# Expert stage of a fused attention, FFN and mixture-of-experts kernel: gated units split before their transpose, down product one tile later

## What is computed

```python
logits = x2d @ gate_kernel                     # 2048 rows, 32 experts
weights, chosen = top_k(softmax(logits), 8)    # weights normed to sum 1
# rows sorted by expert; for the rows of expert e:
inter = silu(rows @ gate_proj[e]) * (rows @ up_proj[e])     # 512 -> 192
out_rows = inter @ down_proj[e]                             # 192 -> 512
x = x + sum over the 8 chosen experts of weight * out_rows
```

## Time and profile before

| what | before |
|---|---|
| runs | 1450.37, 1451.21, 1453.27 us (median 1451.21) |
| span of the profiled execution | 1474.3 us |
| PE busy, share of the span | 1382.7 us, 94% |
| DVE, ACT, POOL busy | 69%, 34%, 26% |
| mean granted TensorE clock | 0.977 |
| DMA | 345.04 MB, 234 GB/s mean |

### The profile page before, as it was taken

How to read it: one execution, slowest core, us unless ns; L and a number is a source line. 1 busy time by engine, 2 the same in 40 slices (tenths; PEclk the granted TensorE clock), 3 DMA queues, 4 the chain that set the end, 5 groups by cost and what they waited for, 6 DMA issues and landing times.

```text
span 1474.3 us, 26984 instructions
## 1 busy us (share of the span) xinstructions
PE 1382.7 (94%) x7525; PEld 753.2 (51%) x7526; DVE 1022.1 (69%) x2467; ACT 505.4 (34%) x916; POOL 383.7 (26%) x313
## 2 busy tenths in 40 slices
PE   4799999999999999999999559999999999999997
PEld 3344444444444444455444236666666666666664
DVE  7879857976895656688776536666666666666664
ACT  1454543444435343422222113333333333333332
POOL 1000000000000000025556543444344344344443
PEclk9899999999999999999999769999999999999999
DMA  9975776766767778836748668889999888989785
GB/s 370 396 262 193 263 256 213 247 197 205 241 209 237 235 254 286 280 119 251 284 195 294 242 227 216 223 218 260 246 246 234 221 229 228 247 223 222 148 162 84
DMA packets 132696, 345.04 MB, mean 234 GB/s; under 512 B 15008, under 2 KB 19616, under 8 KB 125728
## 3 DMA queue, kind: packets, MB, share of 16 engines
q1 hardware_dynamic: 73488, 206.72, 41.6%
q0 software_dynamic: 34640, 85.74, 25.2%
q10 hardware_dynamic: 24512, 51.89, 10.8%
HBM read 192.68 MB, written 151.62 MB: 234 GB/s over the span
## 4 chain that ended last, share of the span: by engine, by line
PE 68%; DVE 16%; DMA 4%; issue 4%; ACT 3%; another core or an unknown queue 2%; ACTq 1%; SPq 1%; DVEq 0%; POOLq 0%
PE PS L1671 17%; PE PS L1673 17%; PE PS L1672 17%; PE PS L1933 5%; PE PS L1961 2%; PE PS L1962 2%; DMA split_experts<-HT 2%; DMA CST<-in_kv 1%; PE PS L1950 1%; DVE EX L1300 1%; PE PS L1951 1%; DVE EX L1306 1%; DVE nw L1027 1%; DMA X<-in_x 1%
## 5 line engine op out<-in xcount | busy, mean ns | idle before, releaser
L587 POOL DMA_INDIRECT out<-BIG,EX x159 | 247.2, 1555 | 354.9 <-issue 153.4
L1671 PE MATMUL PS<-BIG 128*128 (+1 forms) x795 | 269.5, 339 | 5.0 <-DVE BIG L1572 3.3
L1672 PE MATMUL PS<-BIG 128*128 (+1 forms) x795 | 269.5, 339 | 0.0
L1673 PE MATMUL PS<-BIG 128*128 (+1 forms) x795 | 269.5, 339 | 0.0
L1671 PE MATMUL PS<-HT,BIG 128*128 128x512 f16 (+1 forms) x512 | 194.1, 379 | 3.0 <-DVE HT L1101 1.4
L1672 PE MATMUL PS<-HT,BIG 128*128 128x512 f16 (+1 forms) x512 | 194.0, 379 | 0.0
L1673 PE MATMUL PS<-HT,BIG 128*128 128x512 f16 (+1 forms) x512 | 194.0, 379 | 0.0
L560 POOL DMA_INDIRECT rows_by_expert<-HT,POS x128 | 124.9, 976 | 122.6 <-DVE POS L1391 88.1
L1672 PE MATMUL PS<-BIG,EX 128*128 128x512 f16 (+1 forms) x376 | 143.8, 382 | 1.1 <-issue 1.1
L824 ACT ACTIVATE BIG<-PS 128x256 f16<-128x256 f32 x159 | 61.1, 384 | 243.3 <-PE PS L1951 229.0
L1673 PE MATMUL PS<-BIG,EX 128*128 128x512 f16 (+1 forms) x376 | 143.6, 382 | 0.4 <-issue 0.4
(11 more groups left out here) (264 smaller groups left out, 2218.0 us busy)
## 6 DMA issues: line engine op xcount, KB each, us to landing
BIG<-rows_by_expert ACTq DMA_DIRECT2D x159, 280.0 KB
HT<-in_experts SPq DMA_DIRECT2D x64, 640.0 KB, 4.6
BIG<-split_experts SPq DMA_DIRECT2D x32, 1152.0 KB
split_experts<-HT SPq DMA_DIRECT2D x96, 320.0 KB, 2.2
CST<-in_kv SPq DMA_DIRECT2D x64, 256.0 KB, 4.7
split_context<-RT SPq DMA_DIRECT2D x64, 256.0 KB, 4.5
BIG<-split_context SPq DMA_DIRECT2D x7, 2048.0 KB
rows_by_expert<-X SPq DMA_DIRECT2D x32, 280.0 KB
```

Source lines behind the costliest of these rows:

```text
L587: pool.indirect_dma_start(a_out, bass.IndirectOffsetOnAxis(ap=IDY[:, u % V:u % V + 1], axis=0), yt[u % V], None, compute_op=ALU.add).then_ ...
L1671: mm(out, lh, rh, start=first, stop=False)
L1672: mm(out, lh, rl, start=False, stop=False)
L1673: return mm(out, ll, rh, start=False, stop=last_group)
```

## The change

The units are split before they are transposed. `hidden` writes 192 columns once; ACT writes their hi part and DVE their lo part in SBUF (`hidden_hi`, `hidden_lo`), arranged in three blocks of 128 fp16 columns: hi of units 0 to 127; hi of 128 to 191 beside lo of 128 to 191; lo of 0 to 127. PE transposes these three blocks in fp16, and ACT copies them from PSUM to SBUF in one instruction (`hidden_copy`). In `tile_down` the fourth matmul multiplies the stacked middle block with hi weights in both partition halves, and the fifth has 64 rows only. So the last 512 weight columns are kept as hi and as lo (E16 is 5120 columns, 1280 KB per expert), and `split_half` is the same for both halves.

PE's step becomes rows of t + 3, gate and up of t + 2, units of t + 1, down of t. LEAD is 7. ACT's start mixes silu, hi parts and early loads. SP writes eight pads before its loop. `load_counts` reads a table like `load_ints` and takes the maximum with the least value on each register.

```diff
-EL = KC * GU + D
-E16 = EW + EL
+E16 = 2 * EW
-LEAD = 6
+LEAD = 7
+def load_counts(eng, name, table, least, most):
+    loaded = [eng.alloc_register(f"{name}{i}") for i in range(table.shape[-1])]
+    held = [eng.alloc_register(f"{name}_held{i}") for i in range(table.shape[-1])]
+    eng.reg_load(loaded, table)
+    for to, of in zip(held, loaded):
+        eng.reg_alu(to, of, least, ALU.max)
+        eng.free_register(of)
+    return [eng.snap(x, donate=True, min_val=least, max_val=most) for x in held]
...
             def store_half(e, h):
-                nl = (EH, EL - EH)[h]
-                sp.dma_start(dst[:, EW + h * EH:EW + h * EH + nl], eol[:, 0:nl]).then_inc(s_eo, 16)
+                sp.dma_start(dst[:, EW + h * EH:EW + (h + 1) * EH], eol).then_inc(s_eo, 16)
...
-            for e in range(WP):
+            for e in range(2 * WP):
                 pad_expert(e, 16 * e)
             sp.wait_ge(s_tab, 1)
-            with sp.Fori(1, NE // WP) as i:
+            with sp.Fori(1, NE // WP - 1) as i:
                 for h in range(WP):
-                    pad_expert(i * WP + h, i * (16 * WP) + 16 * h)
...
+                    pad_expert(i * WP + (h + WP), i * (16 * WP) + 16 * (h + WP))
+                    replace_expert(i * WP + h, h)
...
             def hidden_hi(t, p):
+                act.wait_ge(s_ea, t + 1)
+                act.activation(es[p][:, 0:M], ea[p], ACT.Copy).then_inc(s_ah2, 1)
+            def hidden_copy(t, p):
                 act.wait_ge(s_at, t + 1)
-                act.activation(eah[p], PS[:, 4, 0:2 * P], ACT.Copy).then_inc(s_ah2, 1)
+                act.activation(eT[p], hT, ACT.Copy).then_inc(s_ac, 1)
...
-            for t in range(1, LEAD):
-                act.wait_ge(s_add[t], LANDED)
-                load_tile(t, 0, rows[t], due[t])
-            tile_hi(1, 1, due[1])
-            tile_silu(0, 0)
+            for t in range(1, 4):
+                load_early(t)
+            tile_silu(0, 0)
+            tile_hi(1, 1, due[1])
+            load_early(4)
+            hidden_hi(0, 0)
+            tile_hi(2, 0, due[2])
+            load_early(5)
+            tile_silu(1, 1)
+            hidden_copy(0, 0)
+            hidden_hi(1, 1)
+            load_early(6)
             with act.Fori(0, LOOPS) as it:
-                rows, due = rows_at("tile_row", it * U + 4, U + 4), experts_due("tile_due", it * U, U + 8)
+                rows, due = rows_at("tile_row", it * U + LEAD, U), experts_due("tile_due", it * U + 3, U + LEAD - 3)
                 for u in range(U):
-                    hidden_hi(t, u % 2)
-                    tile_hi(t + 2, u % 2, due[u + 2])
+                    tile_hi(t + 3, (u + 3) % 2, due[u])
...
-                    tile_silu(t + 1, (u + 1) % 2)
+                    tile_silu(t + 2, u % 2)
+                    hidden_copy(t + 1, (u + 1) % 2)
+                    hidden_hi(t + 2, u % 2)
...
             def split_half(e, h):      # DVE
                 dve.wait_ge(s_eh, e * 2 + (h + 1))
-                if h == 0:
-                    v.scalar_tensor_tensor(eol, est[0], E_S, eoh, ...)
-                else:
-                    v.scalar_tensor_tensor(eol[:, 0:nl], ...)      # 768 columns
-                    v.scalar_tensor_tensor(eoh[ML:P, nl:EH], ...)  # 64 partitions, 512 columns
+                v.scalar_tensor_tensor(eol, est[h], E_S, eoh, ALU.mult, ALU.subtract).then_inc(s_el, 1)
...
             def hidden(t, p):
-                v.scalar_tensor_tensor(ea[p][:, 0:M], ...)
-                v.scalar_tensor_tensor(ea[p][:, M:2 * P], ...).then_inc(s_ea, 1)
+                v.scalar_tensor_tensor(ea[p], PS[:, 2 + p, M:2 * M], ..., eg[p], ...).then_inc(s_ea, 1)
             def hidden_lo(t, p):
-                v.tensor_tensor(eal[p], PS[:, 4, 0:2 * P], eah[p], ALU.subtract).then_inc(s_al2, 1)
+                v.tensor_tensor(es[p][:, M:2 * P], ea[p][:, P:M], es[p][:, P:M], ALU.subtract)
+                v.tensor_tensor(es[p][:, 2 * P:3 * P], ea[p][:, 0:P], es[p][:, 0:P], ALU.subtract).then_inc(s_al2, 1)
...
-                    hidden_lo(t, u % 2)
-                    tile_lo(t + 2, u % 2)
-                    hidden(t + 1, (u + 1) % 2)
+                    tile_lo(t + 3, (u + 3) % 2)
+                    hidden(t + 2, u % 2)
+                    hidden_lo(t + 2, u % 2)
                     weigh(t, u, it * (U // V) + u // V, experts[u])
...
-            def hidden_transpose(p):
-                nc.tensor.transpose(PS[:, 4, 0:P], ea[p][:, 0:P], ident[:, :])
-                nc.tensor.transpose(PS[:, 4, P:2 * P], ea[p][:, P:2 * P], ident[:, :]).then_inc(s_at, 1)
+            def hidden_transpose(t, p):
+                if not isinstance(t, int) or t:
+                    pe.wait_ge(s_ac, t)
+                pe.wait_ge(s_al2, t + 1)
+                for k in range(3):
+                    last = nc.tensor.transpose(hT[:, k * P:(k + 1) * P], es[p][:, k * P:(k + 1) * P], ident16)
+                last.then_inc(s_at, 1)
             def tile_down(t, p, at):
-                pe.wait_ge(s_al2, t + 1)
+                pe.wait_ge(s_ac, t + 1)
...
-                mm(bank, eah[p][:, P:2 * P], stack, start=False, stop=False)
-                mm(bank, eal[p][:, P:2 * P], stack, start=False, stop=True).then_inc(s_ed, 1)
+                mm(bank, eT[p][:, P:2 * P], we[:, bass.ds(at + w1, D)], start=False, stop=False)
+                mm(bank, eT[p][0:ML, P:2 * P], we[0:ML, bass.ds(at + (EW + w1), D)], start=False, stop=True).then_inc(s_ed, 1)
...
             tile_up(0, 0, 0)
             tile_transpose(1, 1, 0)
+            tile_transpose(2, 2, 0)
             pe.wait_ge(s_tab, 1)
+            at = weights_at("first_weights", 0, 4)
+            tile_up(1, 1, at[1])
+            hidden_transpose(0, 0)
             with pe.Fori(0, LOOPS) as it:
-                at = weights_at("tile_weights", it * U, U + 4)
+                at = weights_at("tile_weights", it * U, U + 2)
                 for u in range(U):
-                    tile_transpose(t + 2, (u + 2) % U, it + (u + 2) // U)
-                    pe.wait_ge(s_ea, t + 1)
-                    hidden_transpose(u % 2)
-                    tile_up(t + 1, (u + 1) % 2, at[u + 1])
+                    tile_transpose(t + 3, (u + 3) % U, it + (u + 3) // U)
+                    tile_up(t + 2, u % 2, at[u + 2])
+                    hidden_transpose(t + 1, (u + 1) % 2)
                     tile_down(t, u % 2, at[u])
```

More of the change, by code:

```diff
@@ L263, in build @@
         o += 2 * M
-        ea = [BIG[:, o + i * 2 * P:o + (i + 1) * 2 * P] for i in range(2)]
-        o += 4 * P
-        eah = [f16(BIG, o + i * P, (2 * P,)) for i in range(2)]
-        eal = [f16(BIG, o + (2 + i) * P, (2 * P,)) for i in range(2)]
+        ea = [BIG[:, o + i * M:o + (i + 1) * M] for i in range(2)]
+        o += 2 * M
+        es = [f16(BIG, o + i * M, (2 * M,)) for i in range(2)]
+        o += 2 * M
+        eT = [f16(BIG, o + i * 192, (3 * P,)) for i in range(2)]
         o = [0]
@@ L590, in _ @@
             with pool.Fori(0, LOOPS) as it:
-                start = load_ints(pool, "expert_start", TAB[0:1, 4, bass.ds(it * U, U)], 0, NTILE)
+                start = load_counts(pool, "expert_start", TAB[0:1, 4, bass.ds(it * U, U)], 0, NTILE)
                 for u in range(U):
                     add(it * U + u, u, start[u])
-            start = load_ints(pool, "last_start", TAB[0:1, 4, bass.ds(LOOPS * U, REST)], 0, NTILE)
+            start = load_counts(pool, "last_start", TAB[0:1, 4, bass.ds(LOOPS * U, REST)], 0, NTILE)
             for u in range(REST):
@@ L829, in experts_due @@
             def experts_due(name, t, count):
-                return load_ints(act, name, TAB[0:1, 1, bass.ds(t, count)], 16, 16 * NE)
+                return load_counts(act, name, TAB[0:1, 1, bass.ds(t, count)], 16, 16 * NE)
             def load_tile(u, used, row, pads):
@@ L859, in _ @@
                     if u < TOPK - LEAD:
                         act.wait_ge(s_add[LEAD + u], LANDED)
-                    load_tile((u + LEAD) % U, t + (V + LEAD - U + 1), rows[u + LEAD - 4], due[u + LEAD])
-                    tile_silu(t + 1, (u + 1) % 2)
+                    load_tile((u + LEAD) % U, t + (V + LEAD - U + 1), rows[u], due[u + LEAD - 3])
+                    tile_silu(t + 2, u % 2)
+                    hidden_copy(t + 1, (u + 1) % 2)
+                    hidden_hi(t + 2, u % 2)
@@ L863, in _ @@
             t = LOOPS * U
-            rows, due = rows_at("last_row", t + LEAD, REST - LEAD), experts_due("last_due", t + 2, REST - 2)
+            due = experts_due("last_due", t + 3, REST - 3)
             for u in range(REST):
-                hidden_hi(t + u, u % 2)
+                if u + 3 < REST:
+                    tile_hi(t + u + 3, (u + 3) % 2, due[u])
                 if u + 2 < REST:
-                    tile_hi(t + u + 2, u % 2, due[u])
-                if u + LEAD < REST:
-                    load_tile((u + LEAD) % U, t + u + (V + LEAD - U + 1), rows[u], due[u + LEAD - 2])
```

(24 more changed lines are left out.)

52 lines of the change are left out of this document (23 added, 29 removed).

## The result

The changed kernel takes **1549.75 us** (median of four runs, 1538.91 to 1554.74) against 1450.79 before (1449.69 to 1453.27): ratio 1.0665, 95% interval 1.0625 to 1.0705. It is slower by 99 us, where I forecast 1436.2. A run that lies more than 1.5% above the fastest of its version is named beside the median and left out of the ratio. The profiled execution has a span of 1547.3 us. All of the loss lies in the expert stage. DVE begins to write the tile tables at 825.0 us, and the end is 722 us later; in a clean execution of the old order (experiment 4, its first kernel) that takes 624.5 us.

What follows compares the result with a forecast made beforehand. The prediction took PE to bound the expert stage, with DMA second. Its terms, -8.0 - 5.0 - 3.0 + 1.0 = -15.0 us, carried over to the runs' median of 1451.21, gave 1436.2 us, range 1429 to 1447.

Steps and rivals of the forecast that it cites:

- Down product: Expert stage, PE: five matmuls of 512 columns before and after, the 64-row last one priced as before, 0.22 us: 0.
- One tile more between up and down: Expert stage: PE's room for lo of the units grows, boundary table reads shrink, stalls of 5.7 us mostly go: -5.0 us.
- Transposes of the units: PE, each tile: three fp16 transposes at 0.056 us replace two float32 ones at 0.11: -8.0 us.
- rival B: PE's short transposes: weight load sets their pace; at 0.10 us each 1456.9 (chance 0.04), at 0.08 1447.4 (0.05).
- Start: Start of the expert stage: tile 1's up product runs in PE's 10.54 us gap: -3.0 us, bounds -7 and +2.
- weights: 128 KB more per expert; loading the first four experts takes longer: +1.0 us, bounds 0 and +2.
- end: Stage end: last two down products follow at once, but POOL's last adds give back the 0.85 us won: 0.
- A: Loop boundaries and start: stalls are moved, not removed, leaving only -8.0 and +1.0: 1444.2 us; chance with D, no effect, 0.12.
- C: Fuller half of expert stage: DMA takes over at share 0.99, 4 us not won: 1440 us; chance 0.04.
- The base: Sum made against the profiled span of 1474.3 us, then carried over whole to the runs' median of 1451.21: 1436.2 us.

Runs made afterwards that it cites:

- experiment 4: Kernel before with load_counts: alone (first kernel) 1452.85 us; also with a 64-row last down matmul 1485.02 us; or with ACT's tables shifted off alignment 1583.06 us.
- experiment 1: Changed kernel with 128 rows instead of 64 in the fifth down matmul: 1516.50 us.
- experiment 2: Changed kernel with ACT's two tables shifted by one word, so its loop reads start at multiples of four words: 1473.87 us.
- the version with both mended: Changed kernel with 128 rows in the fifth down matmul and ACT's tables shifted one word: 1435.48 us, in later series 1439.06 and 1436.18.
- experiment 6: The version with both mended, but all six early loads issued before silu, hi and copy at the stage's start: 1442.74 us.
- experiment 5: Kernel before with load_counts, its down product ending in two 64-row matmuls: 1519.87 us; or in one of 96 rows: 1454.25 us.

## Why the prediction was wrong

**Down product: the step that failed first.** I wrote "Five matmuls of 512 columns before and after; the last has 64 rows, and I price it as before, 0.22: 0". I had seen the change of shape and priced it by its columns alone. It costs 0.254 us a tile, so 40 us in steps, and between 32.2 and 38.4 in the time (experiments 1 to 4). A part of the difference is seen: with the shorter step the long steps of experiment 1 sum to 8.0 us more. The bound was missing too: the kernel before has no matmul of 64 rows amid others in this stage, so by the prediction's own rule the cost had to be bounded from both sides.

**One tile more between up and down: the step that failed worst.** I wrote "The boundary read shrinks from 28 numbers to 20 ... That just fits", and priced a read by how many numbers it has. Its start counts: before, the reads start at it*8 + 4 and it*8 + 0, both multiples of four; after, at + 7 and + 3. The 20 numbers take 4.7 us (1.86 + 2.80), not 2.2. The long steps went from 5.7 us to 70.5, which is +64.8 instead of -5.0, and the first step took 10.19 us; in all the starts of the reads cost 75.9 us (experiment 2). The 12 register operations that I had set at 0.5 us a boundary were not measured in this kernel; the 16 of experiment 4 cost some 0.13 us a boundary. With reads that start rightly, the term came out: the long steps of the stage fall to 1.3 us, from 5.7 in the kernel before (-4.4) or from 8.8 in experiment 4's first kernel (-7.5), against the -5.0.

**Transposes of the units: right.** 0.16 us for three, 0.055 each against the 0.056 that I took; rival B is wrong, with its 0.10. So is the Trainium skill's 81 ns ("TensorE: Matmul & The Clock Gate", "Back-to-back issue gap") for this stream. The step of 3.633 is the forecast 3.63, and 0.051 less for 155 steps is -7.9 us (forecast -8.0).

**Start, weights, end.** Compare the version with both mended (span 1435.5) with the kernel before with `load_counts` (1447.6). The first down product comes 4.5 us later (852.7 against 848.2); 2.6 of it is the later start of the tile tables (825.7 against 823.1). Five profiles of the old order have that start at 823.1 to 824.7 us and eight of the new one at 823.2 to 825.7, 0.6 apart in the mean, so the +1.0 for the larger weights is neither shown nor refuted. Of the rest, one more up product now stands ahead of the first down product. That one comes back at the end: the last three steps are 3.20, 2.00 and 1.08 us instead of 3.68, 3.33 and 2.63, 3.4 less, and POOL gives back 1.8 of them (11.8 us from the start of the last down matmul to the end, against 10.0). With steps -7.9, long steps -7.5, the first step +0.3, the last three -3.4, the first down product +4.5 and the end +1.8 the sum is -12.2, and the spans differ by 12.1. So "end: 0" was -1.6, and the start did not win 3 us against this kernel: the gap of 10.5 us that it was to cut belonged to the one profiled execution; in this one it is 4.4. The interleaving was still needed, by experiment 6. That the mended version comes so near to 1436.2 is luck in part: stalls and end won 3.8 us more than forecast, and the start and the weights cost 4.5 where I had them at -2.0.

**The rivals.** A named the right place, ACT's table read that holds up what PE needs, and its sign in the profile, steps of 4.4 us and more. But I bounded it by the 5.7 us of stalls that were there before, as if a stall could only stay. C is seen in two profiled executions of the mended versions, by way of adds that land late, but not by the sign that I gave for it: a DMA share of 0.98 and 0.99 stood before their stalls, and shares of 0.98 and 1.01 (1000 to 1050 us) in the two clean ones came with no step more than 0.5 us too long. None of the rivals ended above 1456.9, for the two prices that mattered had no upper bound at all.

**The base.** Setting the sum against the runs and not the profiled span was right. The 23 us between span and median lay in the profiled execution alone: its attention tiles took 13.7 us, in the other profiles 12.5.

## What to carry to other kernels

Do not put a matmul of 64 rows between matmuls of 128 for the sake of less work: it saves nothing in columns and costs two changes, here 0.25 us in a step of 3.63. Give it 128 rows, as in experiment 1 (with zeros, if the other rows must add nothing; that was not run), or bring several together, as in experiment 5.

Whenever a loop that is unrolled by 8 reads its tables into registers, and the depth of a pipeline changes, look at where each read starts, not only at how much it reads: shift the table so that the start is a multiple of four words, and look at every read that it serves.

When a change alters a shape or an offset that looks like a detail, give it a bound from both sides before giving it a zero; a stall that is small now bounds nothing once its cause can grow.

## What the hardware showed that I had not expected

- **Register reads.** Aligned to four words, 8, 12 and 16 of them took 0.56, 0.79 and 1.02 us: 0.1 us and 0.23 for each group of four. Not aligned, 8, 12 and 16 took 1.86, 2.80 and 3.52: 0.22 to 0.23 for each single word. The Trainium skill ("Runtime: NRT & Kernel Launch", "Instruction fetch mechanics") gives some 200 ns for each register, even in bulk; the unaligned reads agree, the aligned ones take 0.06 to 0.07 us for each. PE's read of 10 words from an aligned start (1.10 us) is slower than its 12 before (0.88): two groups and two single words against three groups.
- **Rows of a matmul.** From 128 to 64 rows and back costs 0.09 to 0.10 us each way at full clock; 96 rows cost nothing.
- **The clock.** Waits of PE of 1.6 to 5.0 us at the boundaries were followed by matmuls at half clock in twelve of 18 cases: 51 us of the stage at 0.50, so some 26 us of the loss came after the waits, not in them.
- **Short transposes.** Three fp16 transposes of 128 columns, each with its own weight load, run 0.055 us apart inside a stream.
